# Keys and values of a group's two sequences made on two column tiles side by side, and spread by twice as many transfers

## The reference

```python
x = x + window_attention(layernorm(x))   # 16 query heads, 2 key/value heads, head size 8, window 32
x = x + butterfly_ffn(layernorm(x))      # expand to 512, butterfly, gelu, butterfly, contract
x = x + linear_attention(layernorm(x))   # phi = elu + 1
x = x + butterfly_ffn(layernorm(x))      # same weights as the first
```

## Time and profile before

| what | value |
|---|---|
| median of three runs | 653.59 us |
| the profiled execution | 652.89 us |
| its span, first to last instruction | 651.1 us |
| TensorE matmuls busy | 610.9 us, 94% |
| VectorE, ScalarE, GpSimd busy | 421.5, 356.0, 304.5 us |
| granted TensorE clock, mean | 1.000 |
| share of the 16 DMA engines, key and value queue included | 9.8% |

### The profile page before, as it was taken

One profiled execution on the slowest core, in us unless ns is written; L12 is line 12 of the kernel. 1 busy time (PEld: TensorE's weight loads), 2 busy tenths in 40 slices (PEclk: granted clock), 3 DMA queues, 4 the chain that ended last, 5 costly groups with the idle time before them and its releaser, 6 DMA issues.

```text
span 651.1 us, 15223 instructions
## 1 busy us (share of the span) xinstructions
PE 610.9 (94%) x5524; PEld 398.8 (61%) x5524; DVE 421.5 (65%) x1131; ACT 356.0 (55%) x539; POOL 304.5 (47%) x584
## 2 busy tenths in 40 slices
PE   3897899999999999999999999999999999998986
PEld 1654557476675656667575657667565666766654
DVE  6388577767666766667676866766676766663340
ACT  1343563656565664755565575656566475546452
POOL 4025172836445562735455472644555373716432
PEclk9999999999999999999999999999999999999999
DMA  9210101011101101110101101110100111000001
GB/s 322 63 22 22 24 19 27 17 26 34 26 19 35 25 20 23 33 26 18 40 20 30 29 17 28 33 24 20 37 21 23 24 31 26 9 11 17 2 18 32
DMA packets 29450, 21.00 MB, mean 32 GB/s; under 512 B 8129, under 2 KB 25153, under 8 KB 29377
## 3 DMA queue, kind: packets, MB, share of 16 engines
q1 hardware_dynamic: 26928, 15.82, 9.8%
q10 hardware_dynamic: 2448, 4.22, 1.8%
HBM read 9.53 MB, written 4.19 MB: 21 GB/s over the span
## 4 chain that ended last, share of the span: by engine, by line
PE 81%; DVE 6%; ACT 5%; issue 4%; POOL 2%; DMA 1%; ACTq 0%; DVEq 0%; POOLq 0%
PE ring L461 17%; PE ring L449 13%; PE ps_t L425 8%; PE ring L383 8%; PE ps_s L409 8%; PE ring L434 5%; PE ring L472 4%; PE ring L492 4%; PE ps_s L404 3%; PE ring L529 3%; ACT L711 2%; PE ring L500 2%; PE ring L481 2%; ACT hid_F L711 2%; PE ring L506 2%
## 5 line engine op out<-in xcount | busy, mean ns | idle before, releaser
L719 ACT ACTIVATE probs_t<-ps_t 128x1024 f32<-128x1024 f32 x64 | 65.4, 1023 | 63.3 <-PE ps_t L425 63.0
L897 DVE TENSOR_REDUCE rowmax<-ps_s 128x16 f32<-128x1024 f32 x64 | 77.7, 1214 | 26.1 <-PE ps_s L409 25.8
L902 DVE TENSOR_TENSOR shifted<-ps_s,rowmax 128x1024 f32<-128x1024 f32 x64 | 78.4, 1225 | 6.7
L425 PEld LDWEIGHTS ps_t<-first,shifted 128*128 128x128 f32 x512 | 55.6, 141 | 29.3 <-issue 27.1
L319 POOL TENSOR_SCALAR rv_F<-mv_F 128x4 f32<-128x4 f32 x16 | 3.6, 227 | 144.7 <-DVE mv_F L875 112.7
L449 PE MATMUL ring<-xT_F,w1b 128*128 128x512 f32 x128 | 63.0, 614 | 8.7 <-ACT hid_F L711 7.9
L425 PE MATMUL ps_t<-first,shifted 128*128 128x128 f32 x512 | 69.1, 278 | 1.2 <-DVE shifted L902 1.2
L409 PE MATMUL ps_s<-kx,q_t 64*32 64x512 f32 x1024 | 66.7, 589 | 0.0
L461 PEld LDWEIGHTS ring<-w,hid_G 128*128 128x128 f32 x512 | 59.5, 192 | 10.2 <-issue 10.2
L449 PE MATMUL ring<-xT_G,w1b 128*128 128x512 f32 x128 | 62.9, 595 | 1.2 <-ACT xT_G L703 0.7
L711 ACT ACTIVATE hid_G<-ring,b 128x512 f32<-128x512 f32 x64 | 42.5, 686 | 39.4 <-PE ring L449 39.2
(11 more groups left out here) (119 smaller groups left out, 1152.9 us busy)
## 6 DMA issues: line engine op xcount, KB each, us to landing
kx<-kv_t SPq DMA_DIRECT2D x128, 40.0 KB, 2.1
x_P<-in_x SPq DMA_DIRECT2D x16, 256.0 KB, 2.8
out_x<-x_G SPq DMA_DIRECT2D x16, 256.0 KB, 2.3
vx_t<-kv_t SPq DMA_DIRECT2D x128, 8.0 KB
up_s<-in_up_m ACTq DMA_DIRECT2D x7, 256.0 KB, 7.7
down_s<-in_down_m ACTq DMA_DIRECT2D x7, 256.0 KB, 7.9
later<-in_later_c SPq DMA_DIRECT2D x1, 648.0 KB, 7.6
u_t<-in_w_exp_t ACTq DMA_DIRECT2D x1, 258.0 KB, 4.8
```

The source lines that it names most:

```text
L425: last = nc.tensor.transpose(ps_t[:, h], shifted[:, j % 2, h].rearrange("p k u -> p (k u)"), ident[:])
L719: nc.scalar.activation(probs_t[:, j % 2], ps_t[:], ACT.Exp).then_inc(drained["T"].sem, 1)
L897: nc.vector.tensor_reduce(rowmax[:, j], s, AX_X, ALU.max).then_inc(vec.sem, 1)
L902: nc.vector.tensor_tensor(shifted[:, j % 2].rearrange("p h k u -> p k h u"), ps_s[:].rearrange("p k (h u) -> p k h u", u=SPAN), m, ALU.sub ...
```

## The change

The product of 32 rows by 512 tokens becomes two of 32 rows by 256 tokens, one for each sequence. The second writes to output partitions 32 to 63, another column tile of the array. kv_t has 64 partitions (32 for each sequence) by 2 tiles by 160 positions. The two copies keep their number and have 64 partitions by 144 elements where they had 32 by 288; the bias is repeated for the second sequence. The source partitions of a transfer now belong to one sequence, so each key and each value transfer becomes two of half the size: 16 key transfers of 16 partitions by 320 positions, and 16 value transfers of 8 partitions by 2 tiles by 64 positions for a group. Which step waits for which is as before.

```diff
-        kv_t = sb("kv_t", [2 * KV * HD, TILES, TSPAN])
+        kv_t = sb("kv_t", [GB * KVR, TPB, TSPAN])
...
-                for h in range(HPK):
-                    sp.dma_start(kx[h:P:HPK, h], kv_t[0:KV * HD].rearrange("d j n -> d (j n)")).then_inc(kx_in.sem, 16)
+                for b in range(GB):
+                    for h in range(HPK):
+                        sp.dma_start(kx[h:P:HPK, h, TPB * TSPAN * b:TPB * TSPAN * (b + 1)],
+                                     kv_t[KVR * b:KVR * b + KV * HD].rearrange("d j n -> d (j n)")
+                                     ).then_inc(kx_in.sem, 16)
...
-                for c in range(4):
-                    for kv in range(KV):
-                        r = KV * HD + kv * HD
-                        sp.dma_start(vx_t[32 * c + kv * HD:32 * c + (kv + 1) * HD, :, kv * SPAN:(kv + 1) * SPAN],
-                                     kv_t[r:r + HD, :, 32 * c:32 * c + SPAN]).then_inc(v_in.sem, 16)
+                for b, c, kv in itertools.product(range(GB), range(4), range(KV)):
+                    r = KVR * b + KV * HD + kv * HD
+                    sp.dma_start(vx_t[32 * c + kv * HD:32 * c + (kv + 1) * HD, TPB * b:TPB * (b + 1), kv * SPAN:(kv + 1) * SPAN],
+                                 kv_t[r:r + HD, :, 32 * c:32 * c + SPAN]).then_inc(v_in.sem, 16)
...
-                nc.tensor.matmul(bank("P.kv")[0:2 * KV * HD, :], wkv_s[:], x_t["P"][:], start=True, stop=True
-                                 ).then_inc(product.sem, 1)
+                for b in range(GB):
+                    last = nc.tensor.matmul(bank("P.kv")[KVR * b:KVR * (b + 1), 0:SEQ], wkv_s[:],
+                                            x_t["P"][:, SEQ * b:SEQ * (b + 1)], start=True, stop=True)
+                last.then_inc(product.sem, 1)
...
-                    last = nc.scalar.activation(
-                        kv_t[:].rearrange("p (b i) n -> p b i n", i=TPB)[:, :, i, to:to + P + PAD],
-                        bank("P.kv")[0:2 * KV * HD].rearrange("p (b n) -> p b n", b=GB)[:, :, first:first + P + PAD],
-                        ACT.Identity, bias=bkv_s[:])
+                    last = nc.scalar.activation(kv_t[:, i, to:to + P + PAD],
+                                                bank("P.kv")[0:GB * KVR, first:first + P + PAD],
+                                                ACT.Identity, bias=bkv_s[:])
```

More of the change, by code:

```diff
@@ L1 @@
+import itertools
 from contextlib import ExitStack
@@ L27 @@
 NG = BATCH * SEQ // TOK
+KVR = 2 * KV * HD
 HID = 512
@@ L83 @@
 UPS = {s: [f"{s}.up{c}" for c in range(CH)] for s in "FG"}
+LAST_GELU = {"F": "F.up1", "G": "G.up1"}
 TURNED = {"P": "P.xT", "W": "F.xT", "F": "L.xT", "L": "G.xT"}
@@ L140, in window_and_linear_attention_with_butterfly_ffn @@
         down_cs = down_co.rearrange("p (s c n) -> p s c n", s=2, c=CH)
-        bkv_s = bkv_all[0:2 * KV * HD]
+        bkv_s = bkv_all[0:GB * KVR]
         spreadb = sb("spreadb", [P, WIN], BF16)
@@ L229, in window_and_linear_attention_with_butterfly_ffn @@
         x_in = Count(sem("x_in"), [("P.x", TRANSFERS["P.x"])], 16)
-        kx_in = Count(sem("kx_in"), [("P.kx", TRANSFERS["P.kx"])], 16 * HPK)
-        v_in = Count(sem("v_in"), [("P.v", TRANSFERS["P.v"])], 16 * 4 * KV)
+        kx_in = Count(sem("kx_in"), [("P.kx", TRANSFERS["P.kx"])], 16 * GB * HPK)
+        v_in = Count(sem("v_in"), [("P.v", TRANSFERS["P.v"])], 16 * GB * 4 * KV)
         y_out = Count(sem("y_out"), [("G.y", TRANSFERS["G.y"])], 16)
@@ L1145 @@
     down_t = down.transpose(0, 1, 3, 2)
-    bkv = np.concatenate([a[_W + "bk"], a[_W + "bv"], np.zeros(P - 2 * KV * HD, np.float32)])
+    bkv = np.concatenate([a[_W + "bk"], a[_W + "bv"], a[_W + "bk"], a[_W + "bv"], np.zeros(P - GB * KVR, np.float32)])
     first = [ident, spread, band, a[_W + "Wq"][:, query_order()], a[_W + "Wk"], a[_W + "Wv"], a[_W + "bq"][query_order()][:, None], bkv[:, None]]
```

## The result

The changed kernel takes 684.75 us (684.05 to 686.35), the kernel before 653.4 us beside it. The ratio is 1.048, with a 95% interval of 1.046 to 1.051: slower by 31.3 us, where 36 were forecast. The profiled execution took 684.05 us with a span of 682.2.

What follows compares the result with a forecast made beforehand. TensorE bounds the kernel, but doubled issues on SP's queue make keys, values and x late: 652.9 + 21.5 (first four intervals) + 14.8 (later turns) = 689.2, with the runs' median 689.9, said as 689 us; range 664 to 704.

Steps and rivals of the forecast that it cites:

- The gain on TensorE: Product on two column tiles side by side: 0.43 us saved a group, 6.9 us in all, if nothing else becomes late.
- The rule on weight loads: Skill's rule on TensorE: loads overlap matmuls only across differing row groups, leaving less than the whole gain; forecast disagreed.
- ScalarE and the first issue: ScalarE's two shorter copies take 0.63 us; the first key issue comes 1.38 us after the product instead of 2.06.
- An issue costs the same at half the size: SP's queue: halved transfers keep their issue cost, 0.59 us a key issue, so twice as many take twice the time.
- The first rival: On SP, half-size transfers issue in little more than half the time (0.42 us); 646.7 us in all, chance 0.09.
- The first four intervals: Product to product, groups 0 to 4: all SP's work decides, adding 7.8, 5.4, 5.5 and 2.8, together 21.5 us.
- The forecast's two paths, by values and by x: Group 1 to 2: next product after 34.0 us by values' landing, 33.4 by next x's, instead of 28.6.
- The later turns: From group 4 on: TensorE waits 1.7 us for keys, a turn costs 1.2 us more; twelve groups, 14.8 us.
- the 16 key issues: SP's key issues for a group: 11.3 us from the doubled mean, 10.1 without long gaps.
- Values and x fitted: From group 4 on: values land 26.1 us and x 27.4 after the product; both just fit and cost nothing.
- The clock's fall: Rival: TensorE's clock falls in the first turns' waits, 1.5 us lost after each of four; 695 us, chance 0.04.

Runs made afterwards that it cites:

- experiments 1: The changed kernel with only the first sequence's key and value transfers, 8 + 8 a group, the second's left out: 647.2 us, ratio 0.990.
- experiment 4: The changed kernel with all 32 transfers, but a semaphore for each sequence's keys, so scores 0 and 1 wait for the first's alone: 675.1 us, ratio 1.033.
- Experiment 7: The kernel with a key semaphore per sequence, plus four useless products ahead of TensorE's wait for values in the first four groups: 670.3 us, ratio 1.026.
- experiment 3: The changed kernel with all 16 key transfers but without the second sequence's value transfers: 680.5 us, ratio 1.041.
- experiment 8: The changed kernel plus three useless products ahead of TensorE's wait for the keys in the first four groups: 685.6 us, ratio 1.050.
- experiment 6: The kernel before with the product on two column tiles, old 8 + 8 transfers, each sequence copied by one overlapping-window instruction: 648.5 us, ratio 0.9925.

## Why the prediction was right

**The gain on TensorE** (0.43 us a group): 0.42 measured in experiments 1 and 4. The rule on weight loads, which the prediction names from the Trainium skill, was rightly set aside. In the changed kernel the passes of both tiles start in pairs (341.31, 341.55), on the same rows of the array.

**ScalarE and the first issue.** 1.38 us after the product was forecast, 1.42 measured (341.31 to 342.73); the two copies take 0.64 where 0.63 was worked out.

**An issue costs the same at half the size.** This carried the forecast. The tile's row of the changed kernel beside the earlier trace rows:

```profile
L280 SPq DMA_DIRECT2D kx<-kv_t x256: 504/589/1797, 16.6 to 579.5; - x128
...
DMA to landing us min/median/max: 1.8/1.9/3.2
```

The median is 589 ns, to the nanosecond that of before. The first rival is gone with it.

**The first four intervals.** Forecast 33.9 for the first, then 34.0 three times, +21.5 us together. Measured 33.8 to 34.3, +21.8. Experiment 7, with no wait for the keys and the clock full, shows the forecast's path alone: values and x make 33.7, 34.0 and 34.0. But they are not the only limit. In experiment 3 half the value transfers are gone, and only the first interval became shorter (29.6); the others were 33.9, 35.3 and 34.0. In these TensorE, held up by the keys and then at the lower clock, comes to the value transposes only 24.9 to 26.4 us after the product, when the values have long landed. The forecast did not have this second limit, so that its sum came within 0.3 us is in part luck. The forecast's two paths, by values and by x, end at nearly the same time in the changed kernel, too. VectorE's and TensorE's timelines in the turn from group 1 to 2, x's moments and the transposes of the values:

```profile
75.05 0.87 DVE L876 BATCH_NORM_STATS2 stats_P<-x_P 128x6 f32<-128x128 f32 x4 [2.26 <-DMA x_P<-in_x]
...
73.17 0.60 PE L388 MATMUL ring<-first,vx_t 128*128 128x128 f32 x4
```

x comes 1.9 us after the transposes begin, and from it to the next product (82.37) are 7.3 us where the transposes have 9.2.

**The later turns: mechanism right, size off.** Forecast +1.2 us a turn, 14.8 in all; measured +0.78, and 0.45 for the last group, 9.0 in all. The term that was mis-sized is the 16 key issues. I had doubled the mean of 5.6 us for 8, long ones included, to 11.3; measured are 10.7 in the mean of the twelve groups, from 10.0 to 11.5. Without a long one 16 issues take 10.0 and 8 take 5.0. So the long ones add 0.7 us to 16 and 0.6 to 8. Before, 8 of the twelve groups had a long issue (over 0.9 us) among their 8 key issues, after, 10 had one among 16: their number has not doubled with the issues. What makes an issue long, no run shows. The other terms held: the first issue came 0.04 later than forecast, and the scores began 1.35 to 1.45 us behind the last issue's end in nine groups and up to 1 us later in three, 1.54 in the mean where 1.5 was taken. The scores come 13.7 us after the product where 14.2 was forecast. That 0.5 us a turn, twelve times, is 5.8 us too much; the first four intervals and group 0's product had 0.3 each too little, which leaves the 5 us by which the sum was too high. Values and x fitted, as forecast: from the scores to the next product are 24.20 us in each of the eleven turns, as before, so it is the keys alone that make them longer.

**Not needed, though foreseen in part.** The clock's fall stood among the rivals as an addition to the forecast, with a chance of 0.04 and 6 us. The fall came, after each of the first four waits for keys (2.4 to 4.6 us), the 6 us did not: experiment 8 shows 0.4 us of it in the changed kernel's time, with two intervals left open. In experiment 4's kernel, where TensorE is the next to be late after the wait, filling the wait gave back 4.8 us (experiment 7).

## What to carry to other kernels

Small transfers in a chain were priced here by their number: count issues, multiply by the row of the same form, and lay the sum beside the user's time to spare, in each phase of the kernel, since the first turns of a pipeline have far less to spare than the steady ones. A saving on the bound engine that doubles the issues of a queue can be had without them: here by bringing both column tiles' results back to the same partitions in the copy, at 648.5 us. When work is added to such a copy, look who reuses its bank.

## What the runs showed of the hardware beyond the forecast

A wait had a price behind itself. In the changed kernel TensorE idles for 4.61 us ahead of the scores at 61.3; that row, and the stretches before, after and later (the granted clock is the column with 1.00, 0.51, 1.00):

```profile
61.31 0.63 PE L409 MATMUL ps_s<-bandb,spreadb 64*32 64x512 bf16 x8 [4.61 <-issue]
...
54.00:58.00 4.00, 2.70 (x21) 1.40 (x19) 3.79 (x15) 1.60 (x2) 0.00 (x0) 1.00 0.12 31
58.50:68.50 10.00, 6.39 (x52) 3.35 (x60) 4.35 (x7) 0.60 (x1) 0.06 (x1) 0.51 0.06 14
69.00:80.00 11.00, 9.91 (x76) 5.56 (x68) 7.76 (x20) 6.26 (x8) 7.24 (x17) 1.00 0.10 27
```

The clock is at the 1.2 GHz level from the wait on and still there in seven microseconds of work behind it. The Trainium skill says the like (TensorE: Matmul & The Clock Gate, HAM oscillation), that waits for transfers between bursts of matmuls halve the clock; the trace agrees, with 1.00 ahead of the wait and 0.51 behind it. The waits of 0.5 to 1.7 us in the later turns left the clock at full speed. Around 2 us the runs show both: it fell behind 2.07 and 2.08 us (experiment 8), and not behind 2.27 and 2.02 us (experiment 7). To fill such a wait with useless products was worth 4.8 us where TensorE was late behind it (experiment 7), and nothing in the changed kernel as a whole (experiment 8).

ScalarE read two overlapping windows of a PSUM bank in one instruction, and the copy of the second sequence wrote the results of output partitions 32 to 63 to partitions 0 to 31. ScalarE's timeline of experiment 6 has both copies:

```profile
312.83 1.00 ACT L760 ACTIVATE kv_t<-ring,first 32x288 f32<-32x288 f32 x2 [1.19 <-PE ring L435]
```

Each takes 0.49 us, as the copies of the same shape before did (0.484).
